# Order of TensorE's work inside a step: a sixth score pair ahead of the transposes, the up products behind it, the third probabilities product beside the output projection

## The chip, the cores and the metric

The kernel runs on one core of one Trainium2 chip. The metric is the device time of one execution in microseconds; the time before is the median of 3 runs, 989.06 us (989.05 to 990.65).

## The reference

The input `x` has 32 items of 256 tokens and width 128. Four layers are added to it in turn, each on a layer norm of `x`:

```python
x = x + attn_a(layernorm(x))   # 16 heads of 8, biases, scale 8**-0.5, corners (0,last) and (last,0) masked
x = x + ffn(layernorm(x))      # gate on the mean over tokens, top 2 of 8 experts, exact gelu, hidden 64
x = x + attn_b(layernorm(x))   # 16 heads of 8, no biases, scale 128**-0.5
x = x + ffn(layernorm(x))
```

`attn` is softmax(q k^T) v per head and an output projection. `ffn` is, for each item, a weighted sum over its two experts of `up(gelu(down(x) + bd)) + bu`.

## The kernel before, in words

`x` stays in SBUF. A turn is one attention over one item, so there are 64 turns: 0 to 31 are attention a, 32 to 63 attention b. One written-out loop (`steps`) runs over steps n = -6 to 70, each cut into 8 parts p = 0 to 7. Every engine has its own list of what it issues in each (n, p); nothing reorders it, and semaphores alone join the lists. A turn is spread over many steps: in step n, norms are taken for turn n+5, q and k projected for n+4, v for n+3, the row maxima found for n+2, the exponentials and the products with the values made for n, and the output of n-1 normalised, transposed and projected.

Short names are used from here on. In step n, for pair p of heads:

- S_p is `max_side(n + 2, p)` (L780 to L792, matmuls at L789): scores for the maxima. VectorE reduces them (L598, `max_done`).
- E_p is `exp_side(n, p)` (L794 to L806, matmuls at L803): transposed scores. ScalarE takes their exp into `probs` (L669, `exp_done`); this is exp_p here.
- W_g is `weigh` (L764 to L778, matmuls at L774): four heads' probabilities times values. W_0, W_1 and W_2 of turn n stand in step n, W_3 in the next.
- mT is the transpose of the split maxima (L886), which waits for GpSimd's split of the maxima (L413 to L419), which waits for the eighth reduction.
- oT is the first transpose of the outputs (L910); oT2 the second (L931), whose result ScalarE copies to `onT` (L739 or L741); wo is the output projection (L959).
- xyT (L943) transposes the normed rows; ScalarE copies its result (L746, L749).

S_p and E_p, and the two feed-forward products, share one PSUM ring of three pairs of banks. The list `uses` (L288) gives the order in which the ring is dealt out, and `fill_pair` (L305) makes a product wait until the use three places earlier has been read: for an S its reduction, for an E its exp, for `down` the four gelus (`h_ready`), for `up` the additions to `x` (`added`). In a step without a feed-forward the order is S0 E0 S1 E1 ... S7 E7, so E_p waits for the reduction of S_(p-1) and S_p for exp_(p-2).

The other transposes and projections share one bank, `m_bank`; `fill_m` (L154) makes each user wait for the reader of the user before it. xyT follows oT2 in that bank, so it waits for the copy to `onT`.

Sixteen steps (`BURSTS`) hold a feed-forward for four turns: `down` (L808, matmuls at L815) in p = 4, four gelus on ScalarE (L722) with a table load before them and one before the next exp, `up` (L819, matmuls at L830 and L838) in p = 5, and two additions on VectorE (L629). There the ring order is ... S3 E3 down S4 E4 up S5 E5 S6 ... . Ten steps (`batch_at(n, 1)`) also run a chain of small VectorE operations for the gate (`weights_of`, `spread`) in p = 5, behind those additions; five of them are burst steps.

Of the kernel before, what the change touches and what calls it, by code (L numbers as in the profile page):

```python
# [55 lines left out]
def build(nc, x_dram_in, attn_w, attn_b, gate_w, down_w, down_b, up_w, up_b, tail_c, ident_c, iota_c, pick_c, out):  # L56
    ctx = ExitStack()
    with ctx:
# [163 lines left out]
        BATCHES = ((0, 8), (8, 8), (16, 8), (24, 8), (32, 8), (40, 8), (48, 4), (52, 4), (56, 4), (60, 4))  # L222
        LATE, FIRST_BY_VECTOR = 56, 56
        BURSTS = (19, 23, 27, 31, 35, 39, 43, 47, 49, 51, 54, 56, 58, 62, 66, 70)
        DOWN_AFTER, UP_AFTER = 3, 4
        MIXING = 12
        WHICH, NBEST = 3, 4
        SPLITS = 5
# [11 lines left out]
        def batch_at(n, after):  # L240

            return next((b for b, (first, rows) in enumerate(BATCHES) if first + rows + BACK - 1 + after == n), None)

        def group_at(n):

            return BURSTS.index(n) if n in BURSTS else None
# [10 lines left out]
        def live(turn):  # L257

            return 0 <= turn < TURNS
# [41 lines left out]
        def pair_of(*use):  # L301

            return ring[place[use] % 3]

        def fill_pair(pe, *use):  # L305

            if place[use] < 3:
                return
            kind, of, p = uses[place[use] - 3]
            if kind == "scores":  # L310
                pe.wait_ge(max_done, of * PAIRS + p + 1)
            elif kind == "exps":
                pe.wait_ge(exp_done, of * PAIRS + p + 1)
            elif kind == "down":
                pe.wait_ge(h_ready, (of + 1) * GROUP)
            else:
                pe.wait_ge(added, (of + 1) * 2)
# [18 lines left out]
        with nc.Block() as block:  # L336
# [320 lines left out]
            def _(act):  # L657
                scalar_opening(act)

                def step(act, n, p):  # L660
# [64 lines left out]
                    if p == 3 and live(n + 3):  # L725
# [6 lines left out]
                        for g in range(IN_SHARE):  # L732
                            last = nc.scalar.copy(of_group((n + 3) % RING, g)[:, :, :, SUMS * g:SUMS * g + HEAD], src[:, g::IN_SHARE])  # L733
                        last.then_inc(v_ready, 1)
                    if p == 4 and live(n - 1):

                        act.wait_ge(oT2_done, (n - 1) + 1)
                        if n - 1 < ITEMS:
                            last = nc.scalar.activation(onT[:, :], m_bank[:, 0:TOKENS], ACT.Identity, bias=wa[:, 514:515])  # L739
                        else:  # L740
                            last = nc.scalar.copy(onT[:, :], m_bank[:, 0:TOKENS])  # L741
                        last.then_inc(onT_ready, 1)
# [8 lines left out]
                    if p == 2 and batch_at(n, 1) is not None:  # L751
# [4 lines left out]
                        nc.scalar.activation(e[rows, :], best[rows, :], ACT.Exp, bias=nbest[rows, :], accum_out=esum[rows, :]).then_inc(exps_done, 1)  # L756

                steps(act, step)

            @block.tensor  # L760
            def _(pe):
                tensor_opening(pe)

                def weigh(turn, g):  # L764

                    pe.wait_ge(exp_done, turn * PAIRS + PER_GROUP // 2 * (g + 1))
                    if g == 0:
                        pe.wait_ge(v_ready, turn + 1)
                        if turn > 0:
                            pe.wait_ge(oT_ready, (turn - 1) + 1)  # L770
                    a, g2 = divmod(g, IN_SHARE)
                    for k in range(TILES):
                        for c in range(PER_GROUP):
                            last = nc.tensor.matmul(values_bank[32 * c:32 * (c + 1), a * TOKENS:(a + 1) * TOKENS],  # L774
                                                    values[turn % RING][:, k, PER_GROUP * g + c, :], probs[g % 2][:, c, k, :],
                                                    start=(g2 == 0 and k == 0), stop=(g2 == IN_SHARE - 1 and k == TILES - 1),
                                                    skip_group_check=True)
                    last.then_inc(pv_done, 1)  # L778
# [15 lines left out]
                def exp_side(turn, p):  # L794

                    r = turn % RING
                    fill_pair(pe, "exps", turn, p)
                    if p == 0:
                        pe.wait_ge(max_in[turn % 2], turn // 2 * 32 + 32)
                    for k in range(TILES):  # L800
                        for a in range(2):
                            rows = slice(BLOCK * a, BLOCK * (a + 1))
                            last = nc.tensor.matmul(pair_of("exps", turn, p)[:, a, k * TOKENS:(k + 1) * TOKENS],  # L803
                                                    k_stack[r][rows, p, k * P:(k + 1) * P], q_stack[r][rows, p, :],
                                                    start=(k == 0), stop=(k == TILES - 1))
                    last.then_inc(t_done, 1)  # L806
# [12 lines left out]
                def up(group):  # L819

                    b = batch_of(group * GROUP)
                    fill_pair(pe, "up", group, 0)
                    pe.wait_ge(split_done, SPLITS * (b + 1))
                    pe.wait_ge(wu_ready, (group + 1) * GROUP)
                    for half in range(2):
                        bank = pair_of("up", group, 0)[:, half, :]
                        for j in range(2):
                            turn = group * GROUP + 2 * half + j
                            col = turn - BATCHES[b][0]
                            nc.tensor.matmul(bank[:, j * TOKENS:(j + 1) * TOKENS].rearrange("p (t d) -> p t d", t=TILES),  # L830
                                             pick[:, col:col + 1].broadcast_to([3 * ITEMS, P]),
                                             biasu_parts[b % 2][:, :].unsqueeze(1).broadcast_to([3 * ITEMS, TILES, WIDTH]),
                                             start=(j == 0), stop=False, skip_group_check=True)
                        for j in range(2):
                            pe.wait_ge(h_ready, group * GROUP + 2 * half + j + 1)
                            for t in range(TILES):
                                at = j * TOKENS + t * P
                                last = nc.tensor.matmul(bank[:, at:at + P], hT[2 * half + j][:, t * P:(t + 1) * P],  # L838
                                                        wu[(group * GROUP + 2 * half + j) % DEEP][:, :],
                                                        start=False, stop=(j == 1 and t == TILES - 1), skip_group_check=True)  # L840
                        last.then_inc(up_done, 1)
# [29 lines left out]
                def step(pe, n, p):  # L871
# [50 lines left out]
                        last.then_inc(v_done, 1)  # L922
                    if p == 5 and live(n):
                        exp_side(n, 4)
                    if p == 5 and group_at(n) is not None:
                        up(group_at(n))
                    if p == 5 and live(n - 1):
# [2 lines left out]
                        for t in range(TILES):  # L930
                            last = nc.tensor.transpose(m_bank[:, t * P:(t + 1) * P], o[:, t, :], ident[:, :])  # L931
                        last.then_inc(oT2_done, 1)
                    if p == 5 and live(n):
                        exp_side(n, 5)
                    if p == 5 and live(n):
                        weigh(n, 1)
                    if p == 6 and (live(n + 5) or live(n - 3)):
# [7 lines left out]
                    if p == 6 and live(n):  # L945
                        exp_side(n, 6)
                    if p == 7 and live(n):
                        weigh(n, 2)
                    if p == 7 and live(n):
                        exp_side(n, 7)  # L950
                    if p == PAIRS - 1 and batch_at(n, 0) is not None:
                        logits(batch_at(n, 0))
                    if p == PAIRS - 1 and live(n - 1):
# [7 lines left out]
                        last.then_inc(wo_done, 1)  # L961

                steps(pe, step)


# [46 lines left out]
```

## Time and profile before

| | |
|---|---|
| median of 3 runs | 989.06 us |
| the profiled execution | 990.56 us |
| its span, first to last instruction | 987.4 us |
| mean granted TensorE clock | 0.982 |
| PE / PEld / DVE busy | 93% / 52% / 80% |
| ACT / POOL busy | 78% / 67% |

PE is TensorE's matmul stream, PEld its weight loads, DVE VectorE, ACT ScalarE, POOL GpSimd. The ends of matmuls are modelled, so distances from start to start say more than busy times. A row of the timeline gives the start, the length, the engine, the line, what it writes and reads, how many instructions were merged in it, and in brackets how long its engine stood idle before it and what ended that.

### The profile page before, as it was taken

How to read it: one execution, taken by the hardware profiler on the slowest of the kernel's cores; microseconds unless marked ns; L12 is line 12 of the kernel's file. 1: busy time of each engine (PE TensorE's matmuls, PEld its weight loads, DVE VectorE, ACT ScalarE, POOL GpSimd, SP SyncE). 2: the span in 40 equal slices, each digit the busy share in tenths (PEclk: the TensorE clock that was granted, in tenths of full speed). 3: DMA queues.
4: the chain of work that ended last, by engine and by line, in shares of the span. 5: the costliest groups of instructions: out<-in, count | busy, mean ns of one | idle time of the engine just before them, and what ended most of it. 6: DMA issues, size and time to landing. Idle time of an engine off the chain costs nothing.

```text
span 987.4 us, 27821 instructions
## 1 busy us (share of the span) xinstructions
PE 917.8 (93%) x10286; PEld 513.9 (52%) x10286; DVE 787.2 (80%) x1394; ACT 772.6 (78%) x1299; POOL 666.2 (67%) x1280
## 2 busy tenths in 40 slices
PE   2589999999999999999999999999999998999885
PEld 1345555545555555555655555555555555654544
DVE  1688888898888888888788887888788878778524
ACT  2168888888888888888888888888888877887863
POOL 8465666667775886768676786768687585764442
PEclk9899999999999999999999999999999999999987
DMA  6577555444444443444444343444444454344001
GB/s 183 150 219 204 154 149 168 141 152 142 135 140 121 150 134 120 145 121 146 119 138 149 121 143 119 153 119 128 136 136 142 125 153 123 118 137 135 5 22 43
DMA packets 144694, 131.66 MB, mean 133 GB/s; under 512 B 9616, under 2 KB 127536, under 8 KB 144432
## 3 DMA queue, kind: packets, MB, share of 16 engines
q1 hardware_dynamic: 143456, 128.49, 43.8%
q8 instruction: 82, 1.34, 0.6%
q10 hardware_dynamic: 1104, 1.41, 0.5%
q14 instruction: 52, 0.43, 0.1%
HBM read 73.76 MB, written 55.57 MB: 131 GB/s over the span
## 4 chain that ended last, share of the span: by engine, by line
PE 67%; ACT 10%; DVE 9%; POOL 5%; issue 4%; DMA 3%; SPq 1%; POOLq 1%; ACTq 1%; DVEq 0%
PE values_bank L774 21%; PE ring L789 11%; PE ring L803 10%; PE m_bank L898 6%; DVE nmax L598 5%; PE m_bank L910 4%; PE m_bank L959 3%; PE m_bank L943 3%; PE m_bank L920 3%; ACT probs L669 2%; PE m_bank L931 2%; ACT hT L722 2%; ACT L713 2%; DMA k_stack<-scratch 2%; DMA scratch<-parts 1%
## 5 line engine op out<-in xcount | busy, mean ns | idle before, releaser
L598 DVE TENSOR_REDUCE nmax<-ring 128x4 f32<-128x1024 f32 x512 | 605.1, 1219 | 98.0 <-PE ring L789 97.0
L669 ACT ACTIVATE probs<-ring 128x1024 f32<-128x1024 f32 x512 | 518.2, 1025 | 54.8 <-PE ring L803 50.4
L774 PE MATMUL values_bank<-probs,values 128*32 128x256 f32 x4096 | 274.9, 386 | 0.7 <-ACT probs L669 0.6
L789 PE MATMUL ring<-k_stack,q_stack 64*128 64x256 bf16 x2048 | 201.2, 277 | 22.7 <-DMA k_stack<-scratch 18.6
L489 POOL TENSOR_SCALAR xy<-x,mv,rstd 128x128 f32<-128x128 f32 x256 | 200.6, 793 | 7.9
L803 PE MATMUL ring<-q_stack,k_stack 64*128 64x256 bf16 x2048 | 189.4, 273 | 8.5 <-DVE nmax L598 7.2
L774 PEld LDWEIGHTS values_bank<-probs,values 128*32 128x32 f32 x4096 | 107.1, 109 | 89.8 <-issue 37.2
L413 POOL TENSOR_SCALAR mparts<-nmax 128x32 bf16<-128x32 f32 x64 | 13.9, 217 | 188.0 <-DVE nmax L598 187.8
L789 PEld LDWEIGHTS ring<-k_stack,q_stack 64*128 64x128 bf16 x2048 | 70.3, 95 | 132.0 <-issue 56.0
L803 PEld LDWEIGHTS ring<-q_stack,k_stack 64*128 64x128 bf16 x2048 | 78.0, 94 | 93.9 <-issue 52.0
L511 POOL TENSOR_TENSOR parts<-rest,parts 128x512 bf16<-128x512 f32 x64 | 74.1, 1158 | 5.4
L505 POOL TENSOR_TENSOR rest<-qk,parts 128x512 f32<-128x512 f32 x64 | 74.1, 1158 | 5.4
L482 POOL TENSOR_TENSOR rstd<-varp,minus_half 128x4 f32<-128x4 f32 (+1 forms) x72 | 69.4, 964 | 6.0
L529 DVE BATCH_NORM_STATS2 raw<-x 128x6 f32<-128x128 f32 x256 | 60.9, 280 | 10.8 <-DMA x<-in_x 10.7
L586 DVE TENSOR_TENSOR x<-x,m_bank 128x256 f32<-128x256 f32 x64 | 27.0, 421 | 49.9 <-PE m_bank L959 49.9
L733 ACT COPY values<-m_bank 128x128 f32<-128x128 f32 x128 | 29.1, 282 | 42.3 <-PE m_bank L920 42.3
L943 PE MATMUL m_bank<-ident,xy 128*128 128x128 f32 x256 | 44.9, 294 | 12.3 <-ACT wb L193 9.0
L696 ACT COPY oT<-values_bank 128x512 f32<-128x512 f32 x64 | 37.4, 585 | 20.1 <-PE values_bank L774 19.0
L502 POOL TENSOR_SCALAR parts<-qk 128x512 bf16<-128x512 f32 x64 | 39.5, 618 | 18.8 <-ACT qk L706 17.2
L746 ACT COPY xnT<-m_bank 128x256 f32<-128x256 f32 x64 | 23.8, 372 | 31.0 <-PE m_bank L943 30.8
L910 PE MATMUL m_bank<-ident,oT 128*128 128x128 f32 x256 | 41.9, 286 | 2.5 <-ACT oT L696 0.8
L508 POOL TENSOR_SCALAR parts<-rest 128x512 bf16<-128x512 f32 x64 | 39.5, 618 | 5.9
(102 smaller groups left out, 1084.0 us busy)
## 6 DMA issues: line engine op xcount, KB each, us to landing
q_stack<-scratch SPq DMA_DIRECT2D x128, 256.0 KB
k_stack<-scratch SPq DMA_DIRECT2D x128, 256.0 KB
scratch<-parts SPq DMA_DIRECT2D x128, 192.0 KB, 2.2
scratch<-parts SPq DMA_DIRECT2D x128, 128.0 KB, 2.2
scratch<-parts SPq DMA_DIRECT2D x128, 64.0 KB, 2.4
out<-x SPq DMA_DIRECT2D x16, 256.0 KB, 2.7
x<-in_x SPq DMA_DIRECT2D x3, 768.0 KB, 7.3
q_stack<-maxT SPq DMA_DIRECT2D x128, 12.0 KB
```

The source lines that it names most:

```text
L482: nc.gpsimd.tensor_tensor(rstd[i][:, both, :], varp[i][:, both, :], minus_half[:, both, :], ALU.pow).then_inc(rstd_done, 1)
L489: last = nc.gpsimd.tensor_scalar(xy[i][:, m, t, :], x[:, (turn % ITEMS) * TILES + t, :], mv[i][:, m, t, 0:1], rstd[i][:, m, t:t + 1], ALU. ...
L505: nc.gpsimd.tensor_tensor(rest[i][:, :, :], qk32[i][:, :, :], parts[i][:, 0], ALU.subtract).then_inc(rest_done, 1)
L511: nc.gpsimd.tensor_tensor(parts[i][:, 2], rest[i][:, :, :], parts[i][:, 1], ALU.subtract).then_inc(parts_ready, 1)
L529: last = nc.vector.bn_stats(raw[i][:, t, :], x[:, (turn % ITEMS) * TILES + t, :])
L598: nc.vector.tensor_reduce(dst, src, axis=AX.X, op=ALU.max, negate=True).then_inc(max_done, 1)
L669: nc.scalar.activation(probs[g % 2][:, c:c + 2, :, :], pair_of("exps", n, p)[:, :, :].rearrange("p x (k q) -> p x k q", k=TILES), ACT.Exp) ...
L774: last = nc.tensor.matmul(values_bank[32 * c:32 * (c + 1), a * TOKENS:(a + 1) * TOKENS], values[turn % RING][:, k, PER_GROUP * g + c, :], ...
L789: last = nc.tensor.matmul(pair_of("scores", turn, p)[:, a, t * TOKENS:(t + 1) * TOKENS], q_stack[z][rows, p, t * P:(t + 1) * P], k_stack[z ...
L803: last = nc.tensor.matmul(pair_of("exps", turn, p)[:, a, k * TOKENS:(k + 1) * TOKENS], k_stack[r][rows, p, k * P:(k + 1) * P], q_stack[r][ ...
L910: last = nc.tensor.transpose(m_bank[:, at:at + P], oT[(n - 1) % 2][:, a, t * P:(t + 1) * P], ident[:, :])
L943: last = nc.tensor.transpose(m_bank[:, at:at + P], xy[(n + 5) % 2][:, m, t, :], ident[:, :])
```

## The change

The ring gives `up` its place after the sixth pair and no longer after the fifth. ScalarE's copy to `onT` moves with it from p = 4 to p = 5, so behind exp_5. On TensorE E_5 moves ahead of `up` and oT2, and E_7 ahead of W_2.

```diff
-        DOWN_AFTER, UP_AFTER = 3, 4
+        DOWN_AFTER, UP_AFTER = 3, 5
...
-                    if p == 4 and live(n - 1):
+                    if p == 5 and live(n - 1):
 
                         act.wait_ge(oT2_done, (n - 1) + 1)
...
                     if p == 5 and live(n):
                         exp_side(n, 4)
+                        exp_side(n, 5)
                     if p == 5 and group_at(n) is not None:
                         up(group_at(n))
                     if p == 5 and live(n - 1):
...
                         last.then_inc(oT2_done, 1)
-                    if p == 5 and live(n):
-                        exp_side(n, 5)
                     if p == 5 and live(n):
                         weigh(n, 1)
...
                     if p == 7 and live(n):
+                        exp_side(n, 7)
+                    if p == 7 and live(n):
                         weigh(n, 2)
-                    if p == 7 and live(n):
-                        exp_side(n, 7)
```

TensorE's order in a step is then S5 E4 E5 [up] oT2 W1 S6 xyT E6 S7 E7 W2 wo, and the ring order in a burst step ... down S4 E4 S5 E5 up S6 E6 S7 E7.

## Rows read from the trace of the kernel before

**Rows 1.** The page's line on engines: busy us, share of the span, instructions.

```profile
PE 917.8 (93%) x10286; PEld 513.9 (52%) x10286; DVE 787.2 (80%) x1394; ACT 772.6 (78%) x1299; POOL 666.2 (67%) x1280
```

**Rows 2.** Timeline of TensorE in step 33 and the start of step 34.

```profile
508.36 0.39 PE L789 MATMUL ring<-k_stack,q_stack 64*128 64x256 bf16 x4
...
509.33 0.39 PE L789 MATMUL ring<-k_stack,q_stack 64*128 64x256 bf16 x4
509.56 0.38 PE L803 MATMUL ring<-q_stack,k_stack 64*128 64x256 bf16 x4
509.94 0.44 PE L931 MATMUL m_bank<-ident,o 128*128 128x128 f32 x2
510.31 0.39 PE L803 MATMUL ring<-q_stack,k_stack 64*128 64x256 bf16 x4
510.63 1.07 PE L774 MATMUL values_bank<-probs,values 128*32 128x256 f32 x16
511.63 0.39 PE L789 MATMUL ring<-k_stack,q_stack 64*128 64x256 bf16 x4
511.95 0.66 PE L943 MATMUL m_bank<-ident,xy 128*128 128x128 f32 x4
...
512.77 0.38 PE L789 MATMUL ring<-k_stack,q_stack 64*128 64x256 bf16 x4
...
514.09 0.39 PE L803 MATMUL ring<-q_stack,k_stack 64*128 64x256 bf16 x4
...
515.28 0.38 PE L803 MATMUL ring<-q_stack,k_stack 64*128 64x256 bf16 x4
515.60 0.39 PE L789 MATMUL ring<-k_stack,q_stack 64*128 64x256 bf16 x4
515.93 0.29 PE L886 MATMUL m_bank<-identb,mparts 128*128 128x128 bf16 x2
```

**Rows 3.** Timeline of VectorE in the same step.

```profile
508.80 2.36 DVE L598 TENSOR_REDUCE nmax<-ring 128x4 f32<-128x1024 f32 x2 [0.34 <-PE ring L789]
...
512.07 2.36 DVE L598 TENSOR_REDUCE nmax<-ring 128x4 f32<-128x1024 f32 x2 [0.24 <-PE ring L789]
```

**Rows 4.** The page's costliest groups: busy us, mean ns of one, idle before.

```profile
L598 DVE TENSOR_REDUCE nmax<-ring 128x4 f32<-128x1024 f32 x512 | 605.1, 1219 | 98.0 <-PE ring L789 97.0
```

**Rows 5.** Timeline of ScalarE in the same step.

```profile
510.04 1.02 ACT L669 ACTIVATE probs<-ring 128x1024 f32<-128x1024 f32 x1 [0.16 <-PE ring L803]
510.96 0.37 ACT L741 COPY onT<-m_bank 128x256 f32<-128x256 f32 x1
```

**Rows 6.** The copy to `onT` in attention a: ns min/median/max, first and last start.

```profile
L739 ACT ACTIVATE onT<-m_bank,wa x32: 467/468/474, 74.6 to 498.1; 128x256 f32<-128x256 f32 x32
```

**Rows 7.** Timeline of TensorE in burst step 43, which also has a batch.

```profile
650.95 0.39 PE L830 MATMUL ring<-biasu_parts,pick 96*128 96x256 bf16 x2
...
653.19 0.38 PE L931 MATMUL m_bank<-ident,o 128*128 128x128 f32 x2
...
653.95 1.07 PE L774 MATMUL values_bank<-probs,values 128*32 128x256 f32 x16
...
657.41 0.39 PE L803 MATMUL ring<-q_stack,k_stack 64*128 64x256 bf16 x4
```

**Rows 8.** Timeline of ScalarE in burst step 43.

```profile
649.35 1.55 ACT L722 ACTIVATE hT<-ring,biasd 128x256 f32<-128x256 f32 x4
...
652.55 1.02 ACT L669 ACTIVATE probs<-ring 128x1024 f32<-128x1024 f32 x1
```

**Rows 9.** Timeline of VectorE in burst step 43.

```profile
655.98 2.32 DVE L598 TENSOR_REDUCE nmax<-ring 128x4 f32<-128x1024 f32 x2
```

**Rows 10.** Timeline of TensorE around its two longest waits in turns 0 to 61.

```profile
804.14 0.27 PE L886 MATMUL m_bank<-identb,mparts 128*128 128x128 bf16 x2 [1.46 <-POOL mparts L419]
...
836.03 0.39 PE L803 MATMUL ring<-q_stack,k_stack 64*128 64x256 bf16 x4 [1.76 <-DVE nmax L598]
```

**Rows 11.** Stretch: us, busy of PE, PEld, DVE, ACT, POOL, granted clock, DMA share, GB/s.

```profile
804.40:807.80 3.40, 3.40 (x27) 1.55 (x27) 0.71 (x2) 1.84 (x3) 3.29 (x4) 0.50 0.48 137
```

## The prediction

> **What bounds the kernel now.** I read the page's shares first: TensorE's matmuls fill 93% of the span, VectorE 80%, ScalarE 78% [rows 1]. Shares can't say who waits last, so I read one plain step (33, period 12.83 us from mT to mT) engine by engine. On TensorE the reader should look at distances between starts [rows 2]. Two bf16 score pairs behind each other are 0.23 us apart (S5 to E4). A score pair followed by an fp32 product is 0.32 ahead of it (E5 to W1, S6 to xyT). W1 takes 1.00, oT2 0.37. Nearly every distance is one of these: TensorE issues without a gap. The exceptions are small: oT2 comes 0.38 after E4, not 0.32, and S1 comes 0.32 after E0, not 0.23, held 0.09 by the exp in its ring place. So TensorE's order sets the period, and each hold that a new order adds counts in full, up to what it takes from another hold.
>
> A second chain is just as tight. VectorE starts a reduction 0.44 after its S (508.36 to 508.80, 511.63 to 512.07) and one takes 1.22 [rows 3, 4]. The eighth ends at 512.07 + 2.36 = 514.43, and mT starts 1.50 later at 515.93, behind GpSimd's split [rows 2, 3].
>
> A handoff to TensorE costs 0.05: the fourth gelu of a burst ends at 649.35 + 1.55 = 650.90 and `up` starts at 650.95 [rows 7, 8].
>
> **The fifth and sixth pair in a plain step.** Nothing is added or removed; the whole change is order. E_5 needs the ring place of S4, so its earliest time is S4 + 0.44 + 1.22 + 0.05 = S4 + 1.71 = 510.07 [rows 2 to 4]. Before, it came at 510.31 and the condition didn't bind. Now it is wanted one pair distance behind E4, at 509.79, and is held 0.28. Then oT2 follows at 510.39, W1 at 510.76, where it was at 510.63: 0.13 later, although one change between bf16 and fp32 (0.32 - 0.23, about 0.1) and the 0.06 hold of oT2 are gone. S6 moves to 511.76.
>
> **The copy to onT.** It now queues behind exp_5. exp_4 starts at 510.04 and the next ScalarE work 0.92 later [rows 5], so exp_5 starts at 510.96, the copy at 511.88 and it ends at 512.25. xyT needs it, at 512.30, where S6 + 0.32 would be 512.08: held 0.22. S7 comes 0.82 behind xyT [rows 2], at 513.12, not 512.77.
>
> **The eighth pair.** E_7 needs the reduction of S6: 511.76 + 1.71 = 513.47. It is wanted at 513.12 + 0.23 = 513.35, so it is held 0.12 and hides the hold of xyT. W2 stands at 513.79, wo at 514.79. Before, E7 to S1 took 1.51 with wo in between [rows 2]; less its own 0.32 and the 0.09 hold, wo to S1 is 1.10. exp_7 now runs earlier and the hold goes. S1 of the next step: 515.89, mT by this path 516.22. By the other: S7 513.12 + 0.44 + 1.22 + 1.50 = 516.28. The later one counts, and mT was at 515.93: **+0.35 us per plain step**. In attention a the copy takes 0.47, not 0.37 [rows 5, 6], so xyT, S7 and mT are 0.10 later: +0.45. Of the 62 steps with both kinds of pairs, 13 are bursts; of the other 49, 25 project q and k of attention a, and I give those 0.45: 25 x 0.45 + 24 x 0.35 = 19.7 us. The bounds for a step: -0.29 if no place in the ring came late (two changes of type and the S1 hold saved), and +0.6 if the 0.28, 0.22 and 0.12 all added up. I take the worked value; its terms are all rows of this one step.
>
> **Bursts.** This is the larger term. The new ring order puts S5 three places behind `down`, so it waits for all four gelus: 650.95. E4 and E5 follow to 651.41. `up` now stands three places behind E4 and so waits for exp_4. That exp can't come early: ScalarE has the gelus, the copy of the values and a table load ahead of it, and it runs from 652.55 to 653.57 [rows 8]. So `up` starts at 653.62, where it started at 650.95 [rows 7]: 2.67 later. Before, `up` was the work that TensorE did during that table load and exp; the cover is gone and TensorE stands idle for some 2.0 us (651.41 + 0.23 to 653.62). From `up` to oT2 are 2.24 [rows 7], and 0.37 more to W1: 656.23 against 653.95, +2.28. E5's 0.32 is saved there and is in that sum. From S6 to the next S1 were 3.97 [rows 2], now 1.71 + 0.32 + 1.00 + 1.10 = 4.13: +0.16. Together **+2.4 per burst**; 8 bursts without the gate's chain: 19.5 us.
>
> In the 5 bursts with that chain (19, 27, 35, 43, 51), VectorE is late as well: additions, gate and the seventh reduction follow each other without idle, and that reduction starts at 655.98 [rows 9]. All move by 2.67, to 658.65, so E_7 comes at 658.65 + 1.22 + 0.05 = 659.92, 2.51 behind its 657.41 [rows 7]; W2 now stands behind it, not ahead, so E7 to S1 is 0.32 + 1.00 + 1.10 = 2.42, not 1.51. +3.4 each: 17.1 us. Three plain steps have the gate's chain too; by the same difference, 1.0 each: 3.0 us.
>
> **Ends.** The last two turns (steps 62, 63) have no S. There xyT waits for a copy that stands one exp later: 0.92 each, 1.8 us. DMA queues, SP and POOL keep their lists; their waits move with the step.
>
> Sum: 19.7 + 19.5 + 17.1 + 3.0 + 1.8 = 61 us.
>
> **The clock.** The longest waits of TensorE before were 1.76 and 1.46 us [rows 10]. The granted clock stayed at full behind the first and was half (0.50, so 1.2 GHz) in the stretch right behind the second [rows 10, 11]. Now 13 bursts have about 2.0 us, with the hold of S5 a little ahead. Half clock for 3.4 us loses at most 1.7 us of TensorE's work; I take 1.5. One fall in two waits: 6.5 x 1.5 = 10 us. The bounds are 0 and 13 x 1.5 = 19.5.
>
> 990.56 + 61 + 10 = 1061.6 for the profiled execution. That one lies 1.50 above the median of the runs, so the median is forecast at **1060 us**.
>
> **A rule of the skill.** The Trainium skill, page Perfetto Trace Analysis, section Identifying the Most-Contended Engine, says that matmul busy time is no good measure of headroom and that the busy share of weight loads is to be read. Loads are at 52% [rows 1]; by that TensorE would have half its time free, and holds of 0.1 to 2 us could vanish in it. The distances in rows 2 speak against it for this kernel. If they did vanish, the time would be 989.
>
> **Rivals.**
> - Holds vanish in slack of TensorE: each step's period is set elsewhere. For: loads 52%. Against: no gaps between starts. 989, chance 3%.
> - The ring releases in time. All hangs on one point: the reduction of S4 done 0.28 earlier than S4 + 1.66, and exp_4 before `up` is wanted. Then the step gains two changes of type and the hold of S1, 0.29: 62 x 0.29 = 18, so **971**, faster. Against it: both releases are read straight from rows 3 and 8. 3%.
> - Only bursts cost, since the 0.28 hold of E_5 and the later S7 are taken up by holds that I did not see: 61 - 19.7 = 41 without falls of the clock, 1030. 9%.
> - As forecast, but the clock never falls: 1050. 24%.
> - As forecast, and it falls in every burst: 1069. 20%.
> - The forecast, some falls: 38%, with its own range 1053 to 1066. What is left, 3%, lies above 1075, if slower bursts also delay the loads of the stacks.
>
> The range is 1040 to 1075: it leaves out 18%. About 0.2% is what a measurement can tell here; faster 3%, the same 3%, slower 94%.
>
> **What would show it.** In plain steps, E5 (L803) 1.71 behind S4 with an idle of PEld "<-DVE nmax L598"; xyT waiting for L741; E7 1.71 behind S6; a period of about 13.2 to 13.4. In bursts, L830 0.05 behind the end of exp_4 and an idle of some 2 us on PE in front of it "<-ACT probs L669"; the burst period near 19.3, and 20.2 with a batch. The row of the clock should show dips in the bursts. I am wrong if L830 still starts right behind the gelus, if plain steps are at 12.8 or less, or if ScalarE or VectorE turn out to set the period with TensorE's holds beside them.

## The result, and the profile after

| | before | after |
|---|---|---|
| median of 4 runs | 989.86 us | 1064.24 us (1062.07 to 1066.76) |
| ratio | | 1.0749, 95% interval 1.0729 to 1.0769 |
| profiled execution / its span | 990.56 / 987.4 us | 1063.2 / 1061.4 us |
| granted clock | 0.982 | 0.965 |

The forecast was 1060 us with a range of 1040 to 1075. Instruction counts are the same in both kernels; the span of the profiled execution grew by 74.0 us.

First the page after: its line on engines, the line of the chain that ended last by engine, and the line on the reductions.

```profile
PE 931.9 (88%) x10286; PEld 535.7 (50%) x10286; DVE 791.7 (75%) x1394; ACT 765.1 (72%) x1299; POOL 666.7 (63%) x1280
PE 61%; ACT 18%; DVE 10%; issue 3%; POOL 3%; DMA 2%; ACTq 1%; SPq 0%; POOLq 0%; DVEq 0%
L598 DVE TENSOR_REDUCE nmax<-ring 128x4 f32<-128x1024 f32 x512 | 609.2, 1220 | 109.3 <-PE ring L789 106.8
```

Every engine's busy share fell [rows 1], and a reduction takes what it took ([rows 4]: 1219 ns, now 1220). In the chain that ended last ScalarE's share rose to 18%, from 10% before. TensorE's busy time grew by 14 us: the matmuls of `up` at L838 take 351 ns in the mean, 279 before, since part of them now runs at half clock (below). The rest of TensorE's 74 us are waits. Which ones, the table of waits after says (engine and line, what it waited for: us in total, times, longest):

```profile
PEld ring L803 <- DVE nmax L598: 72.9, 164, 2.6
DVE x L629 <- PE ring L838: 63.5, 32, 5.1
...
PEld ring L830 <- ACT probs L669: 32.8, 13, 2.5
```

The last row is the wait that the prediction named for `up`: 13 times, 2.5 us each on the weight loads (PEld), behind an exp. The first is E's wait for the reductions; before it was 31.7 us in 60 times. The second is VectorE, which gets the results of `up` later; before it was 15.8 us.

**A plain step.** Timeline of TensorE after, the end of step 33, and below it ScalarE's copy to `onT` in the same step:

```profile
537.39 0.39 PE L789 MATMUL ring<-k_stack,q_stack 64*128 64x256 bf16 x4
...
538.59 0.92 PE L803 MATMUL ring<-q_stack,k_stack 64*128 64x256 bf16 x8
539.43 0.44 PE L932 MATMUL m_bank<-ident,o 128*128 128x128 f32 x2
539.80 1.07 PE L774 MATMUL values_bank<-probs,values 128*32 128x256 f32 x16
540.80 0.39 PE L789 MATMUL ring<-k_stack,q_stack 64*128 64x256 bf16 x4
541.33 0.65 PE L942 MATMUL m_bank<-ident,xy 128*128 128x128 f32 x4
...
542.52 0.39 PE L803 MATMUL ring<-q_stack,k_stack 64*128 64x256 bf16 x4
542.84 1.07 PE L774 MATMUL values_bank<-probs,values 128*32 128x256 f32 x16
```

```profile
540.89 0.38 ACT L741 COPY onT<-m_bank 128x256 f32<-128x256 f32 x1
```

It is the worked step nearly to the hundredth. E4 and E5 are one merged row of eight matmuls that is 0.92 long, where two pairs without a hold take 0.60; inside it E5 starts at 539.11, so 1.72 behind S4 (worked 1.71). S4 to W1 is 2.41 (worked 2.40), and was 2.27 [rows 2]. xyT comes 0.53 behind S6 (worked 0.54) and was 0.32; it starts 0.06 behind the end of the copy to `onT` (541.27), which holds it. E7 comes 1.72 behind S6 (worked 1.71). The period was 12.83 and is 13.14 in undisturbed steps of attention b; worked 13.18. (Undisturbed are the steps away from bursts, gate and logits.)

**A burst.** TensorE, then ScalarE, in burst step 47 after, which has no gate and no half clock around `up`:

```profile
756.13 0.39 PE L830 MATMUL ring<-biasu_parts,pick 96*128 96x256 bf16 x2 [2.24 <-ACT probs L669]
...
758.36 0.38 PE L932 MATMUL m_bank<-ident,o 128*128 128x128 f32 x2
```

```profile
751.45 1.55 ACT L722 ACTIVATE hT<-ring,biasd 128x256 f32<-128x256 f32 x4
752.88 0.47 ACT L733 COPY values<-m_bank 128x128 f32<-128x128 f32 x2
753.75 1.28 ACT L669 ACT_TABLE_LOAD   x1 [0.41 <-PE ring L803]
755.05 1.94 ACT L669 ACTIVATE probs<-ring 128x1024 f32<-128x1024 f32 x2
```

`up` starts 3.13 behind the end of the last gelu (753.00) and 0.06 behind that of exp_4 (755.05 + 1.02); before, it started 0.05 behind the gelus [rows 7, 8]. Its idle time is 2.24 us, not 2.0, and the ScalarE rows say why: 0.41 us of idle time stand **ahead of the table load**. The load belongs to exp_4 and began only once E4 was there. Before, E4 had been issued in time and the load followed the copy at once (step 43: the copy ends at 651.23, the load starts at 651.25). The worked step had the load end where it did before.

**The clock.** Burst step 43 after, the same line 830, and the stretch behind it:

```profile
693.49 0.49 PE L830 MATMUL ring<-biasu_parts,pick 96*128 96x256 bf16 x2 [2.24 <-ACT probs L669]
...
697.36 0.38 PE L932 MATMUL m_bank<-ident,o 128*128 128x128 f32 x2
```

```profile
693.70:697.00 3.30, 3.30 (x18) 3.17 (x17) 0.69 (x1) 0.65 (x1) 0.00 (x0) 0.50 0.02 6
```

From `up` to oT2 are 3.87 us there, against 2.23 in step 47: the second level, 1.2 GHz (0.50), costs 1.6 us. From step 1 to step 61 the trace after has ten half-clock stretches, 44 us together, one in each of ten of the 13 bursts; the trace before has one there [rows 11].

Sorted by kind of step in the two traces, a step being the time from the reduction of its S0 to that of the next S0:

| part | forecast | measured |
|---|---|---|
| plain steps, with the three that hold the gate | 22.7 | 17.1 |
| bursts, without half clock (from the run with fillers below) | 36.6 | 39.1 |
| half clock in bursts | 9.8 | 18.0 |
| ends | 1.8 | -0.2 |
| sum | 71 | 74.0 |

(The one half-clock stretch before lies in burst step 54 and cost 1.6 us there; the 39.1 are net of it. In the run with fillers the bursts have none.)

### The profile page after: what moved, and what is told of

It reads as the page before. It is cut to its first block, busy times and chain, and to the rows that moved or that the text cites. A ratio compares the mean times of both kernels' runs of the same rounds, so it can differ in the third digit from the quotient of the medians.

```text
span 1061.4 us, 27821 instructions
## 1 busy us (share of the span) xinstructions
PE 931.9 (88%) x10286; PEld 535.7 (50%) x10286; DVE 791.7 (75%) x1394; ACT 765.1 (72%) x1299; POOL 666.7 (63%) x1280
## 4 chain that ended last, share of the span: by engine, by line
PE 61%; ACT 18%; DVE 10%; issue 3%; POOL 3%; DMA 2%; ACTq 1%; SPq 0%; POOLq 0%; DVEq 0%
PE values_bank L774 17%; ACT probs L669 10%; PE ring L789 9%; PE ring L803 9%; DVE nmax L598 6%; PE m_bank L898 6%; PE ring L838 4%; PE m_bank L958 4%; PE m_bank L910 3%; PE m_bank L942 3%; PE m_bank L920 2%; ACT hT L722 2%; ACT L669 2%; ACT L713 1%; DMA k_stack<-scratch 1%
## 5 line engine op out<-in xcount | busy, mean ns | idle before, releaser
L598 DVE TENSOR_REDUCE nmax<-ring 128x4 f32<-128x1024 f32 x512 | 609.2, 1220 | 109.3 <-PE ring L789 106.8
L669 ACT ACTIVATE probs<-ring 128x1024 f32<-128x1024 f32 x512 | 505.0, 1025 | 68.7 <-PE ring L803 65.0
L789 PE MATMUL ring<-k_stack,q_stack 64*128 64x256 bf16 x2048 | 200.4, 276 | 29.5 <-DMA k_stack<-scratch 17.1
L803 PE MATMUL ring<-q_stack,k_stack 64*128 64x256 bf16 x2048 | 186.6, 273 | 23.5 <-DVE nmax L598 16.1
L789 PEld LDWEIGHTS ring<-k_stack,q_stack 64*128 64x128 bf16 x2048 | 74.6, 95 | 130.1 <-issue 50.3
L629 DVE TENSOR_TENSOR x<-x,ring 128x512 f32<-128x512 f32 x32 | 22.0, 688 | 63.5 <-PE ring L838 63.5
L838 PE MATMUL ring<-wu,hT 128*128 128x128 f32 x256 | 48.1, 351 | 0.0
```

What stands on the lines that cost most here:

```text
L598: nc.vector.tensor_reduce(dst, src, axis=AX.X, op=ALU.max, negate=True).then_inc(max_done, 1)
L669: nc.scalar.activation(probs[g % 2][:, c:c + 2, :, :], pair_of("exps", n, p)[:, :, :].rearrange("p x (k q) -> p x k q", k=TILES), ACT.Exp) ...
L789: last = nc.tensor.matmul(pair_of("scores", turn, p)[:, a, t * TOKENS:(t + 1) * TOKENS], q_stack[z][rows, p, t * P:(t + 1) * P], k_stack[z ...
```

## The experiments

Each was timed in the same rounds as the kernel before, whose median was 989.9 to 990.6 there. Step lengths are those of each run's profiled execution, against the trace before.

**Plain steps alone.** E5 and E7 ahead, and the copy behind exp_5, only where `group_at(n)` is None.

```diff
                     if p == 5 and live(n):
                         exp_side(n, 4)
+                        if group_at(n) is None:
+                            exp_side(n, 5)
...
-                    if p == 5 and live(n):
+                    if p == 5 and live(n) and not (group_at(n) is None):
                         exp_side(n, 5)
...
+                    if p == 7 and live(n) and group_at(n) is None:
+                        exp_side(n, 7)
                     if p == 7 and live(n):
                         weigh(n, 2)
-                    if p == 7 and live(n):
+                    if p == 7 and live(n) and not (group_at(n) is None):
                         exp_side(n, 7)
```

and on ScalarE, for the copy to `onT`:

```diff
-                    if p == 4 and live(n - 1):
+                    if p == (5 if group_at(n) is None else 4) and live(n - 1):
```

> Only the 49 plain steps of turns 0 to 61 (and the last ones) get the new order: E5 ahead of the transposes of the outputs, E7 ahead of W2, the copy to onT behind exp_5. Burst steps keep the order of before. Theory (ring holds in plain steps, bursts apart): the plain steps of the changed kernel were 0.30 to 0.43 us longer, 17 us in all, so about 1007 us (1003 to 1011). Rival (plain steps cost only because bursts leave the engines out of step, or because the clock fell): within 3 us of before, 987 to 993. Rival (half of the cost is here): 1020 or more.

Measured: 1008.74 us, ratio 1.0192 (1.0168 to 1.0216). The theory holds; plain steps of attention a are +0.41 each, undisturbed ones of attention b +0.31, and the burst steps are unchanged to 0.1 us up to step 51. The rivals, the one of the prediction by which only bursts cost included, are out.

**Burst steps alone**, the complement, with `DOWN_AFTER, UP_AFTER = 3, 5`.

> The complement: only the burst steps get the new order and the new ring place of up; plain steps keep the order of before. Theory: 13 bursts cost 57 us in the changed kernel, so about 1047 us (1041 to 1053), and with a_plain_steps it adds up to the whole. The profile shows up (L830) 0.05 us behind the end of exp_4, TensorE idle for 2.2 us ahead of it, and half clock behind most of these. Rival (the cost of a burst comes from the hold of E5 and the late copy as in plain steps, not from up's wait): 13 x 0.4, so 995.

Measured: 1047.18 us, ratio 1.0570 (1.0544 to 1.0597). The two parts give 18.9 + 57.3 = 76.2 us over before, the whole 74.4: they add up within what the runs tell. The rival is out. The clock differs from run to run: this trace, of the slowest of the five runs (1052.69), has 12 half-clock stretches from step 1 to step 61.

**Only E7 ahead of W2.**

```diff
                     if p == 7 and live(n):
-                        weigh(n, 2)
+                        exp_side(n, 7)
                     if p == 7 and live(n):
-                        exp_side(n, 7)
+                        weigh(n, 2)
```

> Only E7 ahead of W2, in all steps; all else as before. Theory: E7 is held until S6 + 1.71 us, 0.35 behind where it is wanted, W2 and the output projection move by 0.25, 0.09 of it comes back at S1: +0.15 us x 62 steps, 999 us (996 to 1002). Rival (one change between bf16 and fp32 fewer is what counts, the hold is hidden): -0.1 x 62, 984. Rival (nothing, as the chain reduction to GpSimd to mT is unchanged and sets the period): 990.

Measured: 1001.43 us, ratio 1.0107 (1.0080 to 1.0135). TensorE's timeline of this kernel:

```profile
519.79 0.39 PE L789 MATMUL ring<-k_stack,q_stack 64*128 64x256 bf16 x4
...
520.93 0.38 PE L789 MATMUL ring<-k_stack,q_stack 64*128 64x256 bf16 x4
521.51 0.39 PE L803 MATMUL ring<-q_stack,k_stack 64*128 64x256 bf16 x4 [0.20 <-DVE nmax L598]
521.83 1.07 PE L774 MATMUL values_bank<-probs,values 128*32 128x256 f32 x16
```

E7 stands 1.72 behind S6 and 0.58 behind S7, where 0.23 was possible: a hold of 0.35. Each undisturbed plain step is 0.15 longer, in attention a and b alike, as worked. Bursts with the gate are 0.81 longer, since VectorE reduces S6 later there. Alone, this one move costs about half of what an undisturbed plain step loses in attention b (0.15 of 0.31) and over a third in attention a (0.15 of 0.41).

**Fillers for the clock.** The changed kernel, and in bursts ahead of `up`:

```diff
+                    if p == 5 and group_at(n) is not None and live(n) and live(n + 3):
+                        pe.wait_ge(v_ready, (n + 3) + 1)
+                        for f in range(4):
+                            nc.tensor.matmul(m_bank[:, 0:TOKENS], ident[:, :], xnT[(n + 3) % 2][:, :], start=True, stop=True)
```

> The changed kernel with four added fp32 products of 128x256 into the free shared bank, in burst steps between E5 and up, where TensorE stands idle for 2.2 us; their result is not used. They fit into the idle time (about 1.7 us). Theory (the idle time lets the clock fall, 10 of 13 bursts, 1.5 us each): hardly any half-clock stretch in the bursts, 15 us less than the changed kernel, about 1049 us (1045 to 1053). Rival (the stretches have another cause, or half clock costs nothing since others are waited for): 1064, or more by what the products cost.

Measured: 1047.51 us, ratio to before 1.0581 (1.0555 to 1.0606), so 16.7 us less than the changed kernel, with 104 more matmul instructions on TensorE (and as many weight loads). Its timeline in a burst:

```profile
625.49 1.99 PE L929 MATMUL m_bank<-xnT,ident 128*128 128x256 f32 x8
627.81 0.39 PE L830 MATMUL ring<-biasu_parts,pick 96*128 96x256 bf16 x2 [0.32 <-ACT probs L669]
```

`up` comes at the same distance behind the gelus (3.13), so no wait was shortened; only TensorE's idle time was filled, and one half-clock stretch is left of ten, in a plain step. The ten bursts before step 54 fall into two exact kinds: +2.8 to +2.9 without the gate, +3.9 with it. That settles both the share of the clock and the price without it.

**The table load ahead of the wait.** The changed kernel, and behind the copy of the values, in bursts:

```diff
+                    if p == 3 and group_at(n) is not None and live(n):
+                        nc.scalar.activation(spare[:, len(BURSTS) + group_at(n):len(BURSTS) + group_at(n) + 1], bqs[:, :], ACT.Exp)
```

> The changed kernel with one added exp of a 128x1 column in burst steps, behind the copy of the values, so that the table load stands ahead of the wait for E4 and not behind it. Theory (in the changed kernel the table load began 0.41 us behind the copy, only once E4 was there; this is the term that the prediction missed): the load begins right behind the copy, exp_4 starts about 0.2 us earlier (0.41 less the added exp's 0.2), 13 x 0.2 = 3 us less, about 1061 us. Rival (the load waits for something else, or up waits for something else than exp_4): no change in the distance from the last gelu to up, 3.1 us, and 1064.

Measured: 1060.36 us (1056.45 to 1064.07), ratio 1.0703 (1.0662 to 1.0743). The time alone can't tell this from the changed kernel; the profile can. In all 13 bursts `up` starts 2.82 behind the last gelu, not 3.12: 0.30 earlier, where 0.2 were expected. So the load did stand behind the wait, and `up` follows exp_4. TensorE's idle time ahead of `up` is 1.94 us here, and the clock fell as often: ten stretches, 44 us.

**Halved reductions, order of before (control).** The reductions of S4 and S6 read half of the columns; the maxima of those two pairs are then taken over half of the columns only.

```diff
+                        if p in (4, 6):
+                            src = src[:, :, :, 0:P]
                         nc.vector.tensor_reduce(dst, src, axis=AX.X, op=ALU.max, negate=True).then_inc(max_done, 1)
```

> Control for the next two: the order of before, but the reductions of S4 and S6 read only half of the scores (the maxima of two of eight pairs are taken over half of the keys' columns), so they last some 0.65 us and not 1.22. Theory (before, no ring place was late in plain steps, and TensorE's own order sets the period): almost nothing, 983 to 989 us. Rival (VectorE or the chain over GpSimd sets the period by itself): up to 0.5 x 62, so 960.

Measured: 984.94 us, ratio 0.9945 (0.9924 to 0.9966). Undisturbed plain steps are unchanged to 0.01. In the profiled execution the gain is in the three plain steps with the gate, where VectorE is late (0.5 to 0.7 each in steps 11, 55 and 59), and in burst step 54, which is 1.6 shorter because its half-clock stretch did not come.

**Halved reductions, new order in plain steps, copy early.** As plain steps alone, but with the halved reductions, and the copy stays at p == 4.

> Same halved reductions of S4 and S6; in plain steps E5 ahead of the transposes and E7 ahead of W2, but the copy to onT stays ahead of exp_5, and burst steps keep the order of before. Theory (the new order costs by the hold of E5 and E7 on those two reductions; without it two changes between bf16 and fp32 and the hold of S1 are saved): 0.2 to 0.29 us less per plain step than the control, so 10 to 14 us below it, about 975. Rival (the order costs by itself, or changes of type are not dearer): at the control or above it.

Measured: 978.80 us, ratio 0.9886 (0.9870 to 0.9903), 6.1 below the control, where 10 to 14 were expected. The sign is that of the theory: with those two reductions out of the way and the copy early, the new order is the faster one. This is the only kernel here that is ahead of the control too, with the caveat that it leaves out half of the search for the maximum in two of eight pairs. An undisturbed plain step gains 0.21, not 0.29, because the second chain of the prediction takes over:

```profile
507.16 0.38 PE L791 MATMUL ring<-k_stack,q_stack 64*128 64x256 bf16 x4
507.38 0.38 PE L805 MATMUL ring<-q_stack,k_stack 64*128 64x256 bf16 x4
507.69 1.07 PE L776 MATMUL values_bank<-probs,values 128*32 128x256 f32 x16
...
509.79 0.38 PE L791 MATMUL ring<-k_stack,q_stack 64*128 64x256 bf16 x4
509.91 0.24 POOL L419 TENSOR_TENSOR mparts<-mrest,mparts 128x32 bf16<-128x32 f32 x1
510.30 0.27 PE L888 MATMUL m_bank<-identb,mparts 128*128 128x128 bf16 x2
```

(TensorE's timeline of this kernel, with GpSimd's last split; many of its lines lie two further down.) E7 now follows S7 by 0.22, without a hold, but mT comes 0.51 behind S1, not 0.32, and 0.15 behind the end of GpSimd's split of the maxima (510.15), for which it waits. S7's own reduction was not halved. Not all steps gain: the steps with the gate (11 and 59) are 0.9 longer than in the control and the ones behind them some 0.6 shorter. The other part of the shortfall is not worked out.

**The same, with the copy behind exp_5.**

> As the run before it, but the copy to onT stands behind exp_5, as in the changed kernel. Theory (the transposes of the normed rows wait for that copy, S7 comes as late as in the changed kernel, and its reduction and GpSimd's split set mT): the gain is gone, 0.25 to 0.45 us per plain step above the control, about 1000 us (995 to 1006). Rival (only the reductions hold; the copy is hidden): as the run before it, about 975.

Measured: 1001.47 us, ratio 1.0114 (1.0097 to 1.0131). One ScalarE copy moved by one place costs 22.7 us here: the faster order turns slower than before although neither E5 nor E7 waits for a reduction. TensorE's timeline of this kernel shows the wait that is left:

```profile
508.03 0.39 PE L791 MATMUL ring<-k_stack,q_stack 64*128 64x256 bf16 x4
508.96 0.66 PE L947 MATMUL m_bank<-ident,xy 128*128 128x128 f32 x4 [0.55 <-ACT onT L741]
```

xyT comes 0.93 behind S6 and so S7, its reduction, GpSimd's split and mT come late. Undisturbed plain steps are +0.41 in attention a and +0.31 in b, the same as with full reductions (plain steps alone). The late copy is a full second limit.

**Full reductions, copy early.** As plain steps alone, with the copy at p == 4.

> As a_plain_steps (new order in plain steps, full reductions, bursts as before), but the copy to onT stays ahead of exp_5. Theory: without the late copy the transposes of the normed rows are not held and S7 comes 0.2 to 0.3 earlier, but E7 is held by the reduction of S6 all the same, so TensorE's path gives +0.29 us per plain step, not 0.35 to 0.41: 2 to 5 us below the 1008.7 of a_plain_steps, about 1005. Rival (the late copy is the main cause in plain steps): back near 992. Rival (no part of it): 1008 or more.

Measured: 1005.87 us, ratio 1.0160 (1.0140 to 1.0179). Undisturbed plain steps are +0.29 in a and b, to the hundredth what TensorE's path alone was worked to. With the late copy they were 0.41 and 0.31: so the copy adds 0.12 in attention a and 0.02 in b on top of the reductions' hold, because the two holds lie beside each other. The medians of the two runs differ by 2.9 us, less than their intervals can tell apart; the step lengths of the profiles carry this reading.

Four runs with the new order in plain steps can now be laid side by side. Undisturbed plain steps against before, in us, attention a and b:

| | copy early | copy late |
|---|---|---|
| full reductions of S4 and S6 | +0.29, +0.29 | +0.41, +0.31 |
| halved | -0.21, -0.21 | +0.41, +0.31 |

So the step follows the later of two paths. One is TensorE's own, with E5 and E7 behind the reductions. The other is late copy, xyT, S7, its reduction, split, mT; with the late copy it ends last, in the changed kernel too: there mT starts 0.14 behind the end of the split, as with halved reductions, and with the copy early and full reductions 0.31. Taking away the reductions' hold alone gives an undisturbed step nothing back, taking away the late copy alone 0.12 or 0.02, and both together 0.62 or 0.52.

**E5 behind W1**, all else as before: a search for a better order.

> The order of before with one other move: E5 stands behind W1, next to S6, so that one change between bf16 and fp32 is saved where no reduction is waited for. Theory: E5 comes 1.0 us later, so exp_5 does (0.5 to 0.6), S7, which needs it in the ring, is held 0.1 to 0.2, and the saved 0.1 is used up: 0 to +0.1 us per step, 990 to 997. Rival (the change of type is all that counts): -0.1 x 62, 984.

Measured: 992.22 us, ratio 1.0022 (1.0005 to 1.0039). Plain steps are +0.06 each, bursts -0.07. It is no improvement. That the saved change of type is used up by the later exp, as expected, is not shown by itself, but ScalarE's waits for E rose from 50.4 to 83.2 us and those of S for an exp from 39.4 to 57.8 us.

## Why the prediction was right

The mechanism was right in plain steps and bursts, one small term (the ends) was not there, and the number of clock falls was too low. The sum was 3 us short of the growth of the span; so close it came by luck, since errors of both signs cancel: plain steps 5.6 and ends 2.0 too much, bursts 2.5 and half clock 8.2 too little.

- *E5 and E7 held by the reductions of S4 and S6.* Right: 1.71 worked, 1.72 measured for both, +0.15 for E7 alone, +0.29 for both with the copy early. With the copy early the halved reductions turn the sign, which shows this hold as the cause there; with the late copy they change nothing.
- *The copy to onT holds xyT.* Right in place and length (0.54 worked, 0.53 measured). The working had the path through S7 and the split end last, by 0.06 in attention b (516.28 against 516.22); it does, by 0.02 there and by 0.12 in attention a.
- *Plain steps, +0.35 and +0.45.* Measured +0.30 to 0.34 in attention b and +0.41 to 0.43 in a, in undisturbed steps. The term was too large (22.7 for 17.1) because I gave the same price to all 49. The steps behind a burst and those with the logits cost 0.13 to 0.30 only; that they already had holds of their own is an inference. The count of 25 was also taken from the wrong turn: the copy of 0.47 is that of turn n-1, so it stands in 28 plain steps, which is worth 0.3 us.
- *`up` behind exp_4.* Right, with one miss: the table load of exp_4 itself moved by 0.41, as it waits with its exp. +2.8 to 2.9 in place of +2.4 without the gate, +3.9 in place of +3.4 with it.
- *The gate's chain.* The three plain steps with it cost 0.86 to 1.00 in all; the +1.0 on top of a plain step's 0.35 to 0.45 was some 0.4 too much.
- *The ends.* Wrong, and small: 0.92 was worked for each of steps 62 and 63. From the first exp of turn 62 to that of turn 63 took 14.43 before and 14.45 after, and from there to the last exp 8.20 and 8.45. The late copy was hidden there; by what stays open. The -0.2 of the table also holds the start (0.65 shorter).
- *The clock.* I gave half of the bursts a fall of 1.5 us and 10 us in all. Falls came in ten of the 13, 18.0 us in all, so 1.8 each; fillers brought back 16.7 us of the median. The direction was right, the number of falls too low: the row with 1.76 us of idle time and no fall [rows 10] had made me cautious. Every burst has an idle time of 2.24 ahead of `up` and one of 0.49 to 0.85 ahead of S5, 3.1 us earlier. The three bursts without a fall (31, 39 and 47) have them too, so which bursts fall stays open.
- *Slack of TensorE* (the rival from the Trainium skill, page Perfetto Trace Analysis, section Identifying the Most-Contended Engine): not borne out. PEld went from 52% to 50% while the time rose by 7.5%. A low share of weight loads did not mean that holds vanish; the distances between starts were the better sign. (The section names MFU, the matmul work done against the peak, beside that share, and the prediction did not work it out.)
- *The faster rival, 971*: its condition was made true for plain steps by the halved reductions and the early copy, which gave 978.8, 6.1 below the control. So its sign was right under that condition, and GpSimd's chain ended the gain early.

## What to carry to other kernels

In a ring shared by two consumers, write down for each product which use must be free, and when that release comes by the trace, before moving it: an earlier place in the list is worth 0.1 us here and an unmet release costs 0.3 to 2.2 us. The product that fills a table load and an exp on another engine must not be made to wait for that exp. Moving a copy by one place moves every user of the bank that follows it: price it on its own. And where two paths end close together, take each hold away alone and then both before naming a cause.

## What was not expected of the hardware

- In these kernels a table load does not run ahead of its exp's wait: ScalarE is idle for 0.41 us ahead of the load while E4 is awaited, in all 13 bursts; with a tiny exp in front the load began at once and `up` came 0.30 earlier. Whether the engine or the compiled program puts the load there, no run tells.
- Filler matmuls alone, without any wait shortened, were worth 16.7 us of 1064.
- The half clock did not cost half of its length: 44 us of it in the changed kernel and 3 us in the one with fillers lie 15.9 us of span apart, 0.39 us for each us of it (in the bursts alone 18.0 for 44, 0.41).
